# Six PSUM banks in the first round, and expert weights asked for earlier, in a Mamba-style decoder layer

## The chip, the cores and the metric

One core of a Trainium2 chip. The metric is the time of one execution on the device in microseconds (us). The core has five engines that run side by side and meet only at semaphores: TensorE (PE, matrix products, with PEld for its weight loads), VectorE (DVE), ScalarE (ACT), GpSimd (POOL) and SyncE (SP), which issues most of the DMAs. GpSimd issues the gathers, whose rows are chosen by numbers computed on the chip.

## The reference, cut to what matters

The input is x, 4 sequences of 256 tokens with 256 features, 1024 tokens in all. Three blocks follow one another, each with a residual sum and a layer norm:

```python
x = layernorm(x + mixer(x))        # 32 heads of 64, state 128; causal convolution of 4 taps
x = layernorm(x + context_ffn(x))  # 4 experts, chosen by token id
x = layernorm(x + routed_ffn(x))   # 16 experts of width 176, top 2 by router, and 1 shared

def mixer(x):
    x_ssm, z, B, C, dt_raw = split(x @ Win.T)
    dt = softplus(dt_raw + dt_bias)
    xc, Bc, Cc = silu(causal_conv(x_ssm)), silu(causal_conv(B)), silu(causal_conv(C))
    h_t = exp(-dt * exp(A_log)) * h_(t-1) + (dt * xc)_t B_t ;  y_t = h_t C_t
    y = y * rsqrt(mean(y * y) + 1e-6) * silu(z)
    return y @ Wout.T
```

## The kernel before, in words

**The mixer** runs in rounds, one for each pair of heads, 16 pairs. The recurrence is computed as masked attention over blocks of 128 tokens, with decays exp(cum_t - cum_s), where cum is the running sum of dt times the head's rate. A round n has a front and, one and two rounds later, a middle and a tail, so that `step(n, par, front, mid, tail)` of each engine works on three pairs at a time; `steps` calls it for round 0, round 1, a loop over rounds 2 to 15, and two closing rounds.

- Front, TensorE: `project(j)`, j = 0 to 11, is half j % 2 (512 tokens) of tile j // 2. Tiles 0 to 4 are x, B, C, B, C of the pair, tile 5 is the gate z. Each half is six matmuls (L793) into PSUM bank j % 4: the operands are split in a high and a low part. There are eight banks of 512; banks 4 and 5 take turned x and the scores, banks 6 and 7 the mixed output. Before it writes a bank again, TensorE waits in `half_read` until the half four before it has been read: by VectorE's taps, or for z by ScalarE.
- Front, ScalarE: `copy(j)` (L1251) takes a half out of PSUM times the last tap. VectorE: `tap(m, i)` (L1572) adds the three other taps of tile m; tile 0 in six instructions, tiles 1 to 4 in four each. Then ScalarE applies SiLU (L1236): tiles 0 to 3 at the end of its round, tile 4 in the next round, between copy(0) and copy(1), and z (L1242) there too.
- Middle: TensorE turns x to tokens (`x_to_tokens`, L776), scores (L807, L808) and `mix` (L821); GpSimd makes the arguments of the decays (`log_decay`, L477 and L483), ScalarE their exponentials (L1257), VectorE multiplies scores and decays (`weigh`, L1556).
- dt is made once, in round 0: TensorE projects it, ScalarE applies softplus, VectorE takes the running sum (`sum_dt`, L1510, ahead of tile 3's taps), SyncE stores it and loads it back broadcast (L339), TensorE turns dt and cum to tokens (`turn_dt`, L712), and VectorE copies both out (`take_dt`, L1516, L1517). In the kernel before, turning and taking stand between the steps of rounds 0 and 1, and TensorE waits for the copies (semaphore d_dtT) before round 1.

**The output projection** follows, with x1 stored in DRAM.

**The context experts** work on 11 blocks of up to 128 tokens (TBS = 11), sorted by expert. GpSimd gathers the rows of block j (L595); from the fourth on (AHEAD = 3) it waits until TensorE has turned block j - 3. For each block TensorE turns it (L946), multiplies with the chosen context (L955), turns the gate and multiplies again (L977); VectorE adds and takes the statistics. Blocks 0 to 7 (EARLY = 8) are normed by GpSimd (L617), blocks 8 to 10 by VectorE (L1777).

**SyncE's queue** in this stretch is an order written by hand: half of the experts' down weights (`load_down(0)`, L366, 88 partitions of 16 KB), the gate and up weights in four parts (L395, 128 partitions of 11 KB), then the 11 stores of the normed blocks x2 (L399), then the 11 stores of the residual (L403). Ahead of `load_down(0)` it waits for the gathers of all 11 blocks (`ld_row[j]`, L391).

**The shared expert** runs over the same 11 blocks while the router sorts the tokens: TensorE gate and up (L1061), ScalarE SiLU and a copy (L1407, L1412), GpSimd the product (`gate_shared`, L623), TensorE turns it (L1092) and multiplies down (L1111), and GpSimd adds the result to the residual (`add_residual`, L648). The first addition waits until all stores of x2 have landed, because it writes over their source. In the same queue of GpSimd stands the product that prepares the slot table (L655), which waits for VectorE's comparison (L1827). `slot_table` (L1031) on TensorE then gives each slot its token, VectorE writes the list (L1842, semaphore v_tab), and the routed gathers can start.

**The routed experts** work on 24 blocks. GpSimd gathers block j of x2 (`gather_block`, L630), from the fourth on after TensorE has turned block j - 3 (semaphore tx_done). ScalarE's first routed output waits for all 11 residual additions.

## Time and profile before

| | us |
|---|---|
| median of 3 runs | 696.69 (695.76 to 696.72) |
| the profiled execution, its own time | 696.84 |
| its span on the core | 695.1 |
| TensorE busy | 641.2, 92% |
| VectorE busy | 532.2, 77% |
| POOL, ScalarE busy | 475.6, 449.1 |
| mean granted TensorE clock | 0.965 of full |

The profile is of one execution. Times in it count from the start of the span; the 1.7 us between the span and the execution's own time lie around it. A row of a timeline gives start, duration, engine, line, operation, what is written and read, how often, and in brackets how long the engine had been idle and what ended it. The mixer takes the time up to about 500 us, the context experts 519 to 550, the shared expert and the router 550 to 591, the routed experts to 665, and the rest is the combination, the last norm and the stores.

### The profile page before, as it was taken

The page shows a single profiled execution, that of the slowest core. Times are in us where ns is not written, and L with a number is a line of the kernel's source. Part 1 is how long each engine was busy: PE and PEld are TensorE (multiplying, and loading weights), DVE is VectorE, ACT ScalarE, POOL GpSimd, SP SyncE. Part 2 cuts the span into 40 slices and gives each one's busy share as a digit, 9 for nine tenths or more (in the row PEclk, how much of TensorE's full clock was granted, in tenths as well). Part 3 has the DMA queues.
Part 4 walks back from the last instruction along what each step waited for, and adds up shares of the span by engine and source line. Part 5 has one row for each costly group of instructions (what it writes and reads, how often), then busy time and mean ns, then how long its engine had stood idle before and what let it go on. Part 6 is the DMA issues. An engine that isn't in the chain of part 4 may idle for free.

```text
span 695.1 us, 11898 instructions
## 1 busy us (share of the span) xinstructions
PE 641.2 (92%) x3514; PEld 492.9 (71%) x3514; DVE 532.2 (77%) x843; ACT 449.1 (65%) x722; POOL 475.6 (68%) x452
## 2 busy tenths in 40 slices
PE   7699999999999999999999999999998989899920
PEld 5477878878878888788788788788877766455510
DVE  5979999999999999999999999859644566122236
ACT  4657787887887887878878878874224544233321
POOL 4276779888898798798888987586515828444244
PEclk9989999999999999999999999999999999899965
DMA  4222112121131131111211211132252860587334
GB/s 154 90 93 98 62 49 64 42 106 60 46 106 60 46 105 60 47 65 49 99 60 46 106 60 45 56 96 83 69 128 73 233 273 14 143 250 205 90 83 129
DMA packets 25576, 65.07 MB, mean 94 GB/s; under 512 B 4148, under 2 KB 16948, under 8 KB 22812
## 3 DMA queue, kind: packets, MB, share of 16 engines
q1 hardware_dynamic: 22715, 56.96, 24.8%
q0 software_dynamic: 2832, 7.75, 4.3%
q8 instruction: 15, 0.25, 0.2%
q14 instruction: 14, 0.11, 0.1%
HBM read 56.42 MB, written 8.28 MB: 93 GB/s over the span
## 4 chain that ended last, share of the span: by engine, by line
PE 67%; DVE 12%; issue 6%; ACT 5%; DMA 4%; POOL 3%; SPq 2%; POOLq 0%; DVEq 0%; ACTq 0%
PE ps L793 27%; DVE conv L1572 8%; PE ps L821 7%; PE ps L807 5%; PE ps L1071 5%; PE ps L736 3%; PE ps L754 3%; ACT decay L1257 3%; PE ps L1115 3%; DVE decay L1556 3%; PE ps L808 2%; PE ps L776 2%; POOL conv L676 1%; SPq L399 1%; PE ps L955 1%
## 5 line engine op out<-in xcount | busy, mean ns | idle before, releaser
L1572 DVE SCALAR_TENSOR_TENSOR conv<-ps,w_raw,conv 128x506 f32<-128x506 f32 (+3 forms) x352 | 320.3, 933 | 16.9 <-ACT conv L1251 12.2
L793 PE MATMUL ps<-x_hi,w_hi 128*128 128x512 f32 x384 | 159.4, 415 | 6.7 <-DVE conv L1572 5.9
L793 PE MATMUL ps<-x_hi,w_lo 128*128 128x512 f32 x384 | 152.4, 397 | 1.0 <-DVE w_lo L1503 1.0
L1251 ACT ACTIVATE conv<-ps,w_raw 128x512 f32<-128x512 f32 x160 | 108.3, 686 | 69.4 <-PE ps L793 69.2
L793 PE MATMUL ps<-x_lo,w_hi 128*128 128x512 f32 x384 | 151.5, 394 | 0.0
L477 POOL TENSOR_TENSOR decay<-cum_b,cum_tok 128x512 f32<-128x512 f32 (+1 forms) x128 | 103.4, 830 | 15.1 <-DVE cum_tok L1517 15.1
L793 PEld LDWEIGHTS ps<-x_hi,w_hi 128*128 128x128 f32 x384 | 73.1, 190 | 25.5 <-DVE conv L1572 7.9
L483 POOL TENSOR_TENSOR decay<-decay,mask 128x512 f32<-128x512 f32 x64 | 82.5, 1289 | 5.0
L793 PEld LDWEIGHTS ps<-x_hi,w_lo 128*128 128x128 f32 x384 | 72.8, 189 | 18.1 <-DVE w_lo L1503 1.4
L793 PEld LDWEIGHTS ps<-x_lo,w_hi 128*128 128x128 f32 x384 | 73.1, 190 | 13.0
L807 PE MATMUL ps<-conv 128*128 128x256 f32 x256 | 79.5, 392 | 1.7 <-DVE decay L1556 0.3
L1236 ACT ACTIVATE conv<-conv 128x1024 f32<-128x1024 f32 x80 | 79.3, 1057 | 0.0
L1556 DVE TENSOR_TENSOR decay<-ps,decay 128x384 f32<-128x384 f32 x128 | 67.5, 547 | 7.8 <-PE ps L808 7.7
L492 POOL TENSOR_TENSOR y_all<-z_gate,y_all 128x512 f32 (+1 forms) x32 | 41.7, 1303 | 39.3 <-ACT y_all L1270 39.3
L497 POOL TENSOR_TENSOR y_lo<-y_sq,y_hi 128x512 fp32r<-128x512 f32 x32 | 41.5, 1297 | 36.9 <-ACT y_sq L1263 36.9
L1257 ACT ACTIVATE decay<-decay 128x768 f32<-128x768 f32 x64 | 52.0, 837 | 3.9 <-POOL decay L483 3.9
L808 PEld LDWEIGHTS ps<-conv 128*128 128x128 f32 x256 | 48.6, 190 | 6.6
L467 POOL TENSOR_TENSOR w_lo<-w_raw,w_hi 128x1536 fp32r<-128x1536 f32 x15 | 52.5, 3500 | 1.2
L807 PEld LDWEIGHTS ps<-conv 128*128 128x128 f32 x256 | 43.3, 189 | 12.6 <-DVE decay L1556 4.0
L808 PE MATMUL ps<-conv 128*128 128x128 f32 x256 | 49.2, 274 | 0.0
L821 PE MATMUL ps<-decay,xs 128*64 128x256 f32 (+1 forms) x512 | 48.9, 332 | 0.0
L465 POOL TENSOR_TENSOR w_hi<-w_raw,zero 128x1536 fp32r<-128x1536 f32 x15 | 41.2, 2749 | 7.8 <-DVE w_lo L1503 7.8
(259 smaller groups left out, 1095.0 us busy)
## 6 DMA issues: line engine op xcount, KB each, us to landing
cum_b<-cum_scratch SPq DMA_DIRECT2D x16, 1024.0 KB, 4.7
w_raw<-in_winT SPq DMA_DIRECT2D x16, 778.0 KB, 4.4
y_all<-in_wgu SPq DMA_DIRECT2D x4, 1408.0 KB, 19.2
ys_scratch<-y_blk SPq DMA_DIRECT2D x48, 64.0 KB
late<-in_wdn SPq DMA_DIRECT2D x2, 1408.0 KB
x_scratch<-conv SPq DMA_DIRECT2D x19, 128.0 KB, 7.4
late<-in_woutT SPq DMA_DIRECT2D x1, 2048.0 KB, 9.7
res_scratch<-conv SPq DMA_DIRECT2D x11, 130.0 KB
```

The costliest lines, as they stand in the source:

```text
L467: pool.tensor_tensor(w_lo[:, par, :], raw, w_hi[:, par, :].bitcast(F32), ALU.subtract).then_inc(S["w_split"], 1)
L477: pool.tensor_tensor(decay[:, 2 * b:2 * b + 2, c:t], cum_b[:, qp, :, b * T + j * P:(b + 1) * T], cum_tok[:, 2 * b + j, bass.ds(q * 2, 2)]. ...
L483: pool.tensor_tensor(diag, diag, mask[:, :].unsqueeze(1).unsqueeze(1).broadcast_to([P, 2, 2, P]), ALU.add).then_inc(S["p_arg"], 1)
L793: mm = pe.matmul(ps[:, j % 4, :], wp[:, par, w], xp[:, kk, t], start=(i == 0), stop=(i == 5))
L807: pe.matmul(ps[:, 4 + k % 2, 0:T], Bm[:, c0:c0 + P], Cm[:, c0:c0 + T], start=True, stop=True)
L808: pe.matmul(ps[:, 4 + k % 2, T:SC], Bm[:, c1:c1 + P], Cm[:, c1:c1 + P], start=True, stop=True).then_inc(S["s_done"], 1)
L821: mm = pe.matmul(ps[ch, 6 + g, (b % 2) * T + j * P:(b % 2) * T + T], xs[:, 2 * b + j, ch], decay[:, 2 * b + h, c:t], start=(j == 0), stop= ...
L1236: act.activation(conv[:, pp, tile, :], conv[:, pp, tile, :], ACT.Silu).then_inc(S["a_silu"], 1)
L1251: act.activation(conv[:, par, tile, hf * 512:(hf + 1) * 512], ps[:, j % 4, :], ACT.Copy, scale=w_raw[:, par, tap:tap + 1]).then_inc(S["a_c ...
L1257: act.activation(d, d, ACT.Exp).then_inc(S["a_decay"], 1)
L1556: dve.tensor_tensor(decay[:, k, :], ps[:, 4 + k % 2, 0:SC], decay[:, k, :], ALU.mult).then_inc(S["v_m"], 1)
L1572: dve.scalar_tensor_tensor(out=o[:, :, s:], in0=u[:, :, 0:T - s], scalar=w_raw[:, par, c:c + 1], in1=o[:, :, s:], op0=ALU.mult, op1=ALU.ad ...
```

## The change

Round 0 uses six PSUM banks for its tiles, and the turning of dt no longer stops TensorE between rounds 0 and 1; SyncE waits for four gathers where it waited for eleven; and GpSimd's residual additions 8 to 10 move behind the fourth routed gather. The core of the diff:

```diff
+        def tile_bank(n, tile):
+
+            return (0, 2, 6)[tile % 3] if isinstance(n, int) and n == 0 else 2 * tile % 4
...
-            for j in range(TBS):
+            for j in range(AHEAD + 1):
                 sp.wait_ge(ld_row[j], 16)
             load_down(0)
...
-            for j in range(AHEAD):
+            for j in range(NBLK):
                 gather_block(j)
                 if j == 0:
                     gate_shared(TBS - 1)
-                else:
-                    add_residual(TBS - 5 + j)
-            add_residual(TBS - 2)
-            add_residual(TBS - 1)
-            for j in range(AHEAD, NBLK):
-                gather_block(j)
+                elif j == 1:
+                    add_residual(TBS - 4)
+                elif j == 3:
+                    add_residual(TBS - 3)
+                elif j == 4:
+                    add_residual(TBS - 2)
+                    add_residual(TBS - 1)
                 if j >= 9 and j % 2 == 1 and j < 9 + 2 * TB:
                     gather_res((j - 9) // 2)
...
                 mm.then_inc(S["s_dtT"], 1)
-                pe.wait_ge(S["d_dtT"], 1)
...
                 def x_to_tokens(c):
                     ge(pe, S["a_silu"], q * NCONV + 1)
+                    if isinstance(q, int) and q == 0:
+                        pe.wait_ge(S["d_dtT"], 1)
...
                 def project(j):
-                    if j >= 4:
+                    if isinstance(n, int) and n == 0:
+                        if j >= 6:
+                            ge(pe, *half_read(n, j - 6))
+                    elif j >= 4:
                         ge(pe, *half_read(n, j - 4))
-                    elif not (isinstance(n, int) and n == 0):
+                    elif isinstance(n, int) and n == 1:
+                        ge(pe, *half_read(n - 1, j + 6))
+                    else:
                         ge(pe, *half_read(n - 1, j + 8))
...
-                            mm = pe.matmul(ps[:, j % 4, :], wp[:, par, w], xp[:, kk, t],
+                            mm = pe.matmul(ps[:, tile_bank(n, tile) + hf, :], wp[:, par, w], xp[:, kk, t],
...
                 def mix(p, b):
 
                     g = b // 2
+                    if isinstance(p, int) and p == 0:
+                        pe.wait_ge(S["a_z"], g + 1)
...
                 if isinstance(n, int) and n == 0:
                     between[3, 0] = [sum_dt]
+                    between[4, 0] = [take_dt]
...
-            steps(dve, step, take_dt)
+            steps(dve, step)
```

The readers of PSUM (ScalarE's `copy` and `z`, VectorE's `tap`) take `tile_bank` in the same way. In the changed kernel the line numbers are 4 to 13 higher.

VectorE at the end of round 0. Each L1572 or L1585 row is a tap of a tile; a row of 128x4x255 begins a tile, and 128x2x255 begins tile 0 of round 1. Before:

```order
21 L1572 SCALAR_TENSOR_TENSOR conv<-ps,w_raw,conv 128x4x255 [waits a_copy]
22 L1572 SCALAR_TENSOR_TENSOR conv<-ps,w_raw,conv 128x4x254 [waits v_tap]
23 L1572 SCALAR_TENSOR_TENSOR conv<-ps,w_raw,conv 128x2x253 [waits v_tap] x2
24 L1516 COPY dt_tok<-ps 128x256 [waits s_dtT]
25 L1517 COPY cum_tok<-ps 128x256
26 L1572 SCALAR_TENSOR_TENSOR conv<-ps,w_raw,conv 128x2x255 [waits a_copy,d_dtT]
```

Changed:

```order
21 L1529 COPY dt_tok<-ps 128x256 [waits s_dtT]
22 L1530 COPY cum_tok<-ps 128x256
23 L1585 SCALAR_TENSOR_TENSOR conv<-ps,w_raw,conv 128x4x255 [waits a_copy,d_dtT]
24 L1585 SCALAR_TENSOR_TENSOR conv<-ps,w_raw,conv 128x4x254 [waits v_tap]
25 L1585 SCALAR_TENSOR_TENSOR conv<-ps,w_raw,conv 128x2x253 [waits v_tap] x2
26 L1585 SCALAR_TENSOR_TENSOR conv<-ps,w_raw,conv 128x2x255 [waits a_copy]
```

The two copies have moved ahead of tile 4's four taps.

GpSimd where the routed gathers begin (L630 or L634 is a gather, L648 or L652 a residual addition, L623 or L627 the last shared product). Before:

```order
245 L630 DMA xb<-x_scratch,y_all 128x256 [waits v_tab]
246 L623 TENSOR_TENSOR h_tok<-h_tok,u_tok 128x176 [waits a_u]
247 L630 DMA xb<-x_scratch,y_all 128x256
248 L648 TENSOR_TENSOR conv<-conv,y_blk 128x256 [waits a_y]
249 L630 DMA xb<-x_scratch,y_all 128x256
250 L648 TENSOR_TENSOR conv<-conv,y_blk 128x256 [waits a_y] x3
251 L630 DMA xb<-x_scratch,y_all 128x256 [waits tx_done] x7
```

Changed:

```order
247 L634 DMA xb<-x_scratch,y_all 128x256
248 L652 TENSOR_TENSOR conv<-conv,y_blk 128x256 [waits a_y]
249 L634 DMA xb<-x_scratch,y_all 128x256
250 L634 DMA xb<-x_scratch,y_all 128x256 [waits tx_done]
251 L652 TENSOR_TENSOR conv<-conv,y_blk 128x256 [waits a_y]
252 L634 DMA xb<-x_scratch,y_all 128x256 [waits tx_done]
253 L652 TENSOR_TENSOR conv<-conv,y_blk 128x256 [waits a_y] x2
254 L634 DMA xb<-x_scratch,y_all 128x256 [waits tx_done] x5
```

Of the three additions that stood ahead of the fourth gather, one now follows it and two follow the fifth.

## Rows read from the trace of the kernel before

**Rows 1.** The page: busy time, share and instructions of each engine.

```profile
PE 641.2 (92%) x3514; PEld 492.9 (71%) x3514; DVE 532.2 (77%) x843; ACT 449.1 (65%) x722; POOL 475.6 (68%) x452
```

**Rows 2.** Timeline of VectorE, 26 to 75 us: end of round 0, starts of rounds 1, 2.

```profile
28.48 7.95 DVE L1572 SCALAR_TENSOR_TENSOR conv<-ps,w_raw,conv 128x1020 f32<-128x1020 f32 x8
37.66 0.42 DVE L1516 COPY dt_tok<-ps 128x256 f32<-128x256 f32 x1 [1.23 <-PE ps L712]
...
41.79 3.75 DVE L1572 SCALAR_TENSOR_TENSOR conv<-ps,w_raw,conv 128x510 f32<-128x510 f32 x5 [3.38 <-ACT conv L1251]
...
67.64 3.75 DVE L1572 SCALAR_TENSOR_TENSOR conv<-ps,w_raw,conv 128x510 f32<-128x510 f32 x5 [0.51 <-ACT conv L1251]
```

**Rows 3.** Timeline of TensorE, 28 to 75 us: the eleventh half of round 0.

```profile
31.90 0.60 PE L793 MATMUL ps<-x_hi,w_hi 128*128 128x512 f32 x1 [3.36 <-DVE conv L1572]
```

**Rows 4.** Timeline of SyncE's queue, 470 to 600 us: weights and stores of x2.

```profile
540.37 0.32 SPq L366 DMA_DIRECT2D late<-in_wdn  x1
...
543.63 23.07 SPq L399 DMA_DIRECT2D x_scratch<-conv  x11
```

**Rows 5.** Line 399, the stores of x2: time of issue in ns, then the landing.

```profile
L399 SPq DMA_DIRECT2D x_scratch<-conv x11: 320/432/6506, 543.6 to 566.3; - x11
...
DMA to landing us min/median/max: 4.6/14.2/20.3
```

**Rows 6.** Timeline of GpSimd, 505 to 605 us: gathers (L595, L630), addition (L648), product (L655).

```profile
523.14 0.95 POOL L595 DMA_INDIRECT conv<-x_scratch,cum_b  x1 [0.61 <-PE ps L946]
...
526.96 0.95 POOL L595 DMA_INDIRECT conv<-x_scratch,cum_b  x1 [1.19 <-PE ps L946]
...
532.64 0.95 POOL L595 DMA_INDIRECT conv<-x_scratch,cum_b  x1 [1.22 <-PE ps L946]
...
571.30 0.72 POOL L648 TENSOR_TENSOR conv<-conv,y_blk 128x256 f32<-128x256 f32 x1 [5.91 <-DMA x_scratch<-conv]
...
575.95 2.60 POOL L655 TENSOR_TENSOR y_all<-y_all,cum_b 128x1056 bf16<-128x1056 f32 x1
...
586.34 1.06 POOL L630 DMA_INDIRECT xb<-x_scratch,y_all  x1 [0.55 <-DVE y_all L1842]
...
593.66 0.96 POOL L630 DMA_INDIRECT xb<-x_scratch,y_all  x1 [0.16 <-issue]
```

**Rows 7.** Timeline of TensorE, 549 to 606 us: shared expert, slot table, third routed block.

```profile
573.61 0.42 PE L1092 MATMUL ps<-ident,h_tok 128*88 128x128 f32 x2 [3.26 <-POOL h_tok L623]
...
584.72 0.88 PE L1031 MATMUL ps<-y_all,conv 128*64 128x48 bf16 x44
...
595.83 0.69 PE L1045 MATMUL ps<-ident,xb 128*128 128x128 f32 x2 [1.72 <-DMA xb<-x_scratch,y_all]
```

**Rows 8.** Timelines of GpSimd and ScalarE, 26 to 75 us: decay arguments and exponentials.

```profile
38.55 1.61 POOL L477 TENSOR_TENSOR decay<-cum_b,cum_tok 128x512 f32<-128x512 f32 x2 [15.09 <-DVE cum_tok L1517]
...
48.70 1.57 ACT L1257 ACTIVATE decay<-decay 128x768 f32<-128x768 f32 x2
```

**Rows 9.** Timeline, 0 to 45 us: SyncE asks for the running sums.

```profile
30.45 0.81 SPq L339 DMA_DIRECT2D cum_b<-cum_scratch  x2
```

**Rows 10.** The page, DMA issues: count, size, median us from issue to landing.

```profile
cum_b<-cum_scratch SPq DMA_DIRECT2D x16, 1024.0 KB, 4.7
```

**Rows 11.** DMA queues, 518 to 540 us: packets, MB, share; then landing.

```profile
q0 software_dynamic: 528, 1.44, 23.8%
...
conv<-x_scratch,cum_b POOLq DMA_INDIRECT x11, 3.3
```

**Rows 12.** Timeline of VectorE, 564 to 700 us: the comparison that the product at 575.95 needs.

```profile
571.32 1.83 DVE L1827 TENSOR_TENSOR y_all<-y_all,cum_b 128x1056 f32<-128x1056 int32 x1
```

**Rows 13.** DMA queues, 540 to 570 us, weights and stores: packets, MB, share.

```profile
q1 hardware_dynamic: 2237, 8.63, 87.6%
```

**Rows 14.** Busy time by stretch: PE, PEld, DVE, ACT, POOL; then clock, DMA share, GB/s.

```profile
546.00:552.00 6.00, 6.00 (x40) 5.27 (x39) 3.32 (x11) 2.19 (x5) 4.79 (x15) 1.00 1.01 223
552.00:558.00 6.00, 5.30 (x33) 3.86 (x31) 2.37 (x6) 5.57 (x11) 4.80 (x6) 1.00 0.99 410
```

More of the change, by code:

```diff
@@ L1241, in z @@
                         ge(act, S["v_y"], q * 2 - 2)
-                    act.activation(z_gate[:, qp, hf * 512:(hf + 1) * 512], ps[:, (2 * NCONV + hf) % 4, :], ACT.Silu
+                    act.activation(z_gate[:, qp, hf * 512:(hf + 1) * 512], ps[:, tile_bank(q, NCONV) + hf, :], ACT.Silu
                                    ).then_inc(S["a_z"], 1)
@@ L1250, in copy @@
                     tap = KD * PW + tile * TAPS + TAPS - 1
-                    act.activation(conv[:, par, tile, hf * 512:(hf + 1) * 512], ps[:, j % 4, :], ACT.Copy,
+                    act.activation(conv[:, par, tile, hf * 512:(hf + 1) * 512], ps[:, tile_bank(n, tile) + hf, :], ACT.Copy,
                                    scale=w_raw[:, par, tap:tap + 1]).then_inc(S["a_copy"], 1)
@@ L1568, in tap @@
                     o = conv[:, par, m, :].rearrange("p (b t) -> p b t", b=NB)[:, 2 * halves.start:2 * halves.stop, :]
-                    u = ps[:, (2 * m) % 4:(2 * m) % 4 + 2, :].rearrange("p a (b t) -> p (a b) t", b=2)
+                    u = ps[:, tile_bank(n, m):tile_bank(n, m) + 2, :].rearrange("p a (b t) -> p (a b) t", b=2)
                     u = u[:, 2 * halves.start:2 * halves.stop, :]
```

## The prediction

> **What bounds the kernel now.** I read the page first: TensorE is busy for 641.2 of 695.1 us, VectorE for 532.2 [rows 1]. A share near full says little about an edit, so I went to the two places the diff touches and asked there which wait ends last.
>
> The first is the hand-over from round 0 of the mixer (the first pair of heads) to round 1. VectorE runs round 0's last eight taps from 28.48 to 36.43, copies the turned step sizes out of PSUM (37.66 to 38.41, two copies of 0.42 us that overlap a little), and then stands still: its first tap of round 1 is at 41.79 [rows 2]. In between TensorE turns dt and waits for those copies before it projects anything of round 1. TensorE, for its part, stood idle for 3.36 us before 31.90, waiting for taps to free a PSUM bank, and came back at a matmul of 0.60 us [rows 3]. From 41.79 on VectorE has no gap until 67.64, where it waits 0.51 us for ScalarE [rows 2]: a start of round 1 that is earlier on VectorE is earlier for everything behind it, round by round.
>
> The second is the stretch from the context experts to the routed ones. SyncE holds the 7 MB of expert weights (one of 1408 KB, then four) until all eleven context gathers have landed, at 540.37, and puts the eleven stores of x2 behind them in the same queue, from 543.63 to 566.7 [rows 4]. A store takes up to 20.3 us to land, and one took 6.51 us to issue, since the queue was full [rows 5]. The chain that ended last runs straight through this issue. GpSimd's first residual addition waits for it, 5.91 us, until 571.30 [rows 6]; the shared expert's products queue behind it, and TensorE idles 3.26 us before 573.61 [rows 7].
>
> **The change, part by part.**
>
> *Six banks in round 0, dt turned without a stop.* No matmul, copy or tap is added or removed. With six banks TensorE's seventh to twelfth half of round 0 wait for taps two halves older; VectorE was never the one that waited there, so its taps still end when they did: 36.43, plus the two copies, now between tile 3 and tile 4 (37.66 to 38.41, 0.75 us). That is 37.2. Round 1's first two halves need only tile 3's taps (about 32) and run while VectorE does tile 4. Even at the slow clock's 0.43 us per matmul the first is done by 34.5, so ScalarE's copy is there before 37.2. The second copy stands behind a SiLU that needs tile 4's last tap: 37.2 + 1.06 + 0.69 = 39.0, and VectorE wants it after three taps of 0.75 us, at 39.5. So VectorE's first tap moves from 41.79 to 37.2: **-4.6 us**. Who could be late next? GpSimd's decay arguments of round 0 started at 38.55, on VectorE's copy [rows 8]; now they can start when the cumulative sums are back, which SyncE asks for at 30.45 and has 4.7 us later [rows 9, 10], at 35.2, 3.3 us earlier. That is less than 4.6, but ScalarE takes the first pair, ready 2.9 us after GpSimd's start, only at 48.70 [rows 8]: cover enough. The z wait that the change puts ahead of the first mix is met about 20 us before it. Bounds: -3.5 (if a slow clock holds round 1's third and fourth half, which VectorE meets by 42.2) to -5.0.
>
> *Weights behind four gathers: what it frees.* The fourth gather is issued at 523.14 [rows 6] and lands 3.3 us later [rows 11], so the weights start at 526.5 instead of 540.4, 13.9 us earlier. The first store stood behind all of them and landed at 543.6 + 20.3 = 563.9, so they are in by about 550 now, and the last x2 store goes out as soon as its block is normed. GpSimd's first addition no longer waits; but not all of the 5.91 us comes back. The product at 575.95 (2.60 us) waits for VectorE's comparison that ends at 573.15 [rows 12], whatever the stores do; it then starts 2.8 us earlier, the shared expert's loop of 2.27 us per block follows it, and the slot table, at 584.72 and long waited for [rows 7], comes at about 581.6. So the first routed gather, 586.34 [rows 6], moves by **-3.1 us**. Bounds: -1.5 to -5.9.
>
> *What it costs.* Six gathers, of blocks 5 to 10, now fly among 7 MB of weights. No row of before shows a gather beside a backlog like that. What the rows do show: eleven gathers made 528 packets [rows 11], 48 each, three on each of the 16 DMA engines; the weights and stores made 2237, one for each row [rows 13]. While the down weights move, in rows of 16 KB, the queues carry 223 GB/s, and later, with gate and up in rows of 11 KB, 410 [rows 14]: 1.2 and 0.44 us for a row on one engine. If each packet of a gather waits for one row of weights, a gather costs 3 x 1.2 = 3.6 us more in the first stretch (some 10 us, 528 to 540 with the gathers' own time) and 1.3 in the second. Gather 5 is issued at 526.96 and lands at 530.3; block 5 has been turned when gather 8 goes out, at 532.64 [rows 6], so its slack is 1.9 us, and 2.7 for the later ones. Gather 5 comes at 533.9, 1.7 late. Gather 6 follows 3.6 + 0.5 us behind, at 538.0, where 534.3 was needed: 3.7. Gather 7 is at 541.0 for 536.5: 4.5. After that a gather takes 1.8 us in a cadence of 2.17 (1.22 idle and 0.95 of issue [rows 6]) and no more is lost. Everything behind is **+4.5 us** later. The lower end is 0: later, among copies of expert weights, 18 gathers never made TensorE wait. The upper end is every gather held until the weights are in: 550 against 534.3, +16. I take the middle reading, since it rests on counted packets.
>
> At this place a rule of the Trainium skill speaks against the change. The Trainium skill, page "DMA: Bandwidth & Descriptors", section "Queues, rings and completion order", has an engine drain a packet of typically 9 to 17 descriptors from one ring before it turns to another. By that rule the wait at each turn would be a whole load's share, and the sum would end above the time before; the packet counts of this trace, one per row, speak for the shorter turn, and no row here shows the two queues both backed up.
>
> *Fourth routed gather ahead of three additions.* It was issued at 593.66 [rows 6], behind three additions of 0.7 us each; it will go out about 1.8 us earlier. TensorE waits there for the third gather alone, 1.72 us before 595.83 [rows 7]; the fourth lands at 597.0 as it is, while TensorE is still at the third's work. The delayed additions have room too, as ScalarE's first routed output, which waits for them, comes some 7 us later. I cost it at **0**, bounds -0.3 and +0.3; if the third gather came earlier, the fourth would be next.
>
> Sum: -4.6 - 3.1 + 4.5 + 0 = **-3.2 us**. Against the profiled execution's own 696.84 (span 695.1, 1.7 around it) that is 693.6; the median of the runs is 0.15 lower, so 693.5.
>
> **The rivals.**
> 1. *Gathers are not held up* (below 1.5 us): -7.7, 689.0. For it: the later gathers among weight copies. Against: those copies are 528 KB at a time, with pauses, not 7 MB in a row.
> 2. *Whole loads go first*, the slower side. Place: blocks 5 and 6 of the context experts. If each of gather 5's three packets waits for a load's share (1408 KB at 223 GB/s is 6.3 us, at 410 it is 3.4), it lands at 530.3 + 13.1 = 543.4; gather 6 waits for the other two and lands near 550.3, where 534.3 was needed: +16, so 696.7 - 7.7 + 16 = 705.0. It decides once the loss passes 9.1 us. The rule of the Trainium skill above would do this.
> 3. *In between* (6.3 to 9.1 us lost): within 0.2% of before.
> 4. *The bank edit does not pay*, because some wait keeps VectorE's second round at 41.79: 693.5 + 4.6 = 698.1. I see no such wait.
>
> **How the numbers follow.** Forecast (loss of 1.5 to 6.3 us) 0.50; rival 1 0.20; rival 2 0.17; rival 3 0.10; rival 4 0.03. A measurement of this kernel can tell about 0.2%, 1.4 us, from no change. Faster: 0.50 + 0.20 = 0.70. Same: 0.10 + 0.03 = 0.13. Slower: 0.17. The range goes from 688.8 (all gain, nothing lost) to 699.5, which takes in rivals 3 and 4 and the mild end of rival 2; most of rival 2 and bank gains beyond the sum are left out. The forecast's own range is 690.5 to 695.3.
>
> **What would show it.** VectorE's first tap of round 1 near 37.2, and the context stage starting 4.6 us earlier. The weights' issue some 14 us earlier still, right behind the fourth gather. Gather landings of 5 to 8 us in place of 3.3, with TensorE waiting for them between blocks 5 and 8; 3.3 would be rival 1, over 12 rival 2. No wait of GpSimd for an x2 store, and TensorE's 3.26 us gone. It is wrong if round 2 does not start 4.6 us earlier, or if the product at 575.95 moves by less than the stores do.

## The result and the profile after

The changed kernel is slower. Its median is 699.15 us (19 runs, 696.15 to 704.69) against 695.25 us (19 runs, 691.61 to 698.18) of the kernel before on the same chips; the ratio is 1.0066, 95% interval 1.0048 to 1.0084. Of 695.25 us that is 4.6 us more (the two medians differ by 3.9). The forecast was 3.2 us less. Put on the 696.69 us that it started from, the measured ratio gives 701.3, where it had 693.5 and a range up to 699.5. The profiled execution of the changed kernel happens to be one of its quick ones: 697.0 us, span 695.1, the same span as in the profile of before. So the trace shows a draw, in which a gain and a loss cancel, and the loss of the median has to be found with the experiments.

The page's busy times answer to [rows 1]:

```profile
PE 638.4 (92%) x3514; PEld 490.8 (71%) x3514; DVE 531.6 (76%) x843; ACT 449.7 (65%) x722; POOL 475.1 (68%) x452
```

**The start of round 1.** VectorE's timeline of the changed kernel (start, duration, engine, line, operation, count, idle before). Tap code is at L1585 now, the copies at L1529 and L1530:

```profile
33.13 0.42 DVE L1529 COPY dt_tok<-ps 128x256 f32<-128x256 f32 x1
33.46 0.42 DVE L1530 COPY cum_tok<-ps 128x256 f32<-128x256 f32 x1
33.91 7.68 DVE L1585 SCALAR_TENSOR_TENSOR conv<-ps,w_raw,conv 128x1020 f32<-128x1020 f32 x9
41.51 0.68 DVE L1560 TENSOR_TENSOR xs<-ps,dt_tok 128x512 f32<-128x512 f32 x1
...
63.65 3.75 DVE L1585 SCALAR_TENSOR_TENSOR conv<-ps,w_raw,conv 128x510 f32<-128x510 f32 x5 [0.51 <-ACT conv L1264]
```

The nine taps at 33.91 are the last four of round 0 and the first five of round 1, without a gap between them; the first one of round 1 begins at 37.85, where the forecast had 37.2. The standstill of 3.38 us before 41.79 [rows 2] is gone. The wait for ScalarE that stood at 67.64 is at 63.65.

**The context stage.** GpSimd's context gathers (L599) of the changed kernel. The first is at 515.04, where it was at 518.87 before; the sixth, of block 5, is the one at 522.34:

```profile
515.04 1.18 POOL L599 DMA_INDIRECT conv<-x_scratch,cum_b  x1 [21.86 <-DMA x_scratch<-conv]
...
522.34 0.95 POOL L599 DMA_INDIRECT conv<-x_scratch,cum_b  x1 [0.67 <-PE ps L959]
...
526.99 0.95 POOL L599 DMA_INDIRECT conv<-x_scratch,cum_b  x1 [1.22 <-PE ps L959]
535.70 0.95 POOL L599 DMA_INDIRECT conv<-x_scratch,cum_b  x1 [7.76 <-PE ps L959]
539.40 0.95 POOL L599 DMA_INDIRECT conv<-x_scratch,cum_b  x1 [2.75 <-PE ps L959]
541.56 0.95 POOL L599 DMA_INDIRECT conv<-x_scratch,cum_b  x1 [1.22 <-PE ps L959]
```

SyncE and TensorE beside them:

```profile
522.38 0.32 SPq L370 DMA_DIRECT2D late<-in_wdn  x1
522.74 2.83 SPq L399 DMA_DIRECT2D y_all<-in_wgu  x4
```

```profile
534.74 0.69 PE L959 MATMUL ps<-ident,conv 128*128 128x128 f32 x2 [6.08 <-DMA conv<-x_scratch,cum_b]
```

The weights are queued 0.04 us after gather 5 was begun. TensorE then stands for 6.08 us, and GpSimd, which waits for TensorE before it can issue gather 8, for 7.76. The chain of work that ended last has the gather's own time (start, duration, what), and the answer for line L599 the landings of all eleven:

```profile
522.34 12.36 DMA conv<-x_scratch,cum_b
534.70 0.04 issue
534.74 0.69 PE ps L959 x2
```

```profile
DMA to landing us min/median/max: 2.7/6.3/12.4
```

Before, all eleven took 3.3 us. The wait has a second price: TensorE's clock fell to half during it (532 to 538, rows at the end of this document), so block 5 took 4.0 us from its turn at 534.74 to the next one, where a block takes 2.2. From the first context gather to the last it was 536.97 - 518.87 = 18.1 us; it is 541.56 - 515.04 = 26.5 now, so 8.4 us were lost where the forecast had 4.5.

How the two queues shared the DMA engines can be read from the single packets. A gather is 48 of them: 32 rows of 4 KB and 16 closing packets of 4 bytes, so two rows and a closing packet on each of 16 engines. Gather 4, issued at 520.73, has its packets from 522.43 to 523.12. Gather 5, issued at 522.34, begins its first row only at 529.07. The queues (kind: packets, MB, share of 16 engines) from 523.2 to 529, and then from 529 to 532.6; q1 carries the weights and q0 the gathers:

```profile
q1 hardware_dynamic: 83, 1.22, 94.0%
```

```profile
q1 hardware_dynamic: 54, 0.72, 87.4%
q0 software_dynamic: 52, 0.15, 19.6%
```

First weights alone moved, then about one packet of weights for each packet of a gather. The records do not name the engine of a packet, but each begins where another one ends. Joined that way, most engines that carry w_dn read: five rows of w_dn, a row of the gather, a row of w_dn, a row of the gather, a row of w_dn, the gather's closing packet, a row of w_dn. Gather 5 lost 5.0 us before its first row (it began 6.7 us after the issue, gather 4's 1.7 us), 2.8 in the turns from first to last packet (3.5 against 0.7), and 1.8 until the last of its sixteen landing signals, one from each engine. Fifteen of them had come by 533.58; the one at 534.70 is from an engine where a packet of 16 KB of instructions (queue q8) had come in between.

**From there to the routed experts.** GpSimd's first residual addition, the shared expert's product and the first routed gather, to be laid beside [rows 6]:

```profile
571.12 0.73 POOL L652 TENSOR_TENSOR conv<-conv,y_blk 128x256 f32<-128x256 f32 x1
...
579.44 2.53 POOL L659 TENSOR_TENSOR y_all<-y_all,cum_b 128x1056 bf16<-128x1056 f32 x1 [1.93 <-DVE y_all L1841]
...
589.24 1.06 POOL L634 DMA_INDIRECT xb<-x_scratch,y_all  x1 [0.55 <-DVE y_all L1856]
```

The addition has no wait for a store any more (5.91 us before). But the product that follows now waits for VectorE. From the last context gather to the first routed one it is 47.7 us, after 49.4, so 1.7 us less. Most of that is the clock: before, TensorE was at half its clock for 3.4 us of this stretch (from 574.9), and in the changed kernel never. The kernel with the order alone (below), which has no relief of the stores and no such fall, needs 48.0, and the one with early weights alone, with relief and a fall of 3.4 us, needs 49.3. At like clock, as far as single traces can tell, 0.1 to 0.3 of the 5.91 us are left. VectorE's comparison, which the product waits for, starts 36.5 us behind the last context gather (578.10), where it was 34.4 (571.32).

**The routed stage** is 2.9 us shorter than before (695.1 - 589.24 = 105.9 against 108.8). The granted clock goes with it. TensorE's stretches (busy time and count of each engine, then PEclk, DMA share, GB/s), of before and then of the changed kernel:

```profile
596.00:598.00 2.00, 1.60 (x6) 0.66 (x8) 0.00 (x0) 0.38 (x1) 0.95 (x1) 0.50 1.00 270
598.00:600.00 2.00, 2.00 (x9) 0.76 (x6) 0.07 (x1) 0.32 (x1) 0.00 (x0) 0.50 0.51 162
600.00:602.00 2.00, 2.00 (x9) 0.92 (x9) 0.69 (x2) 0.38 (x1) 0.94 (x1) 0.50 0.00 0
```

```profile
596.00:598.00 2.00, 1.57 (x10) 0.50 (x6) 0.34 (x1) 0.52 (x2) 1.83 (x3) 1.00 0.93 264
598.00:600.00 2.00, 1.09 (x8) 0.50 (x8) 0.00 (x0) 0.19 (x1) 1.84 (x3) 1.00 0.82 241
600.00:602.00 2.00, 1.41 (x10) 0.56 (x8) 0.56 (x2) 0.70 (x2) 1.04 (x2) 1.00 0.73 209
```

Before, TensorE had stood for 1.72 us at 595.83 [rows 7] and then ran 6 us at 1.2 GHz, with matmuls of 0.79 us in place of 0.46. The changed kernel stood twice for 0.2 to 0.3 us there and kept 2.4 GHz. The other traces bear this out: the nine of the experiments below without such a fall near its start have 104.6 to 105.7 us for it, whatever the order of the gathers, and those with a fall of 3.4 us 105.7 to 107.8.

### The profile page after: what moved, and what is told of

Same layout as the page of the kernel before. It is cut to its first block, busy times and chain, and to the rows that moved or that the text cites. A ratio compares the mean times of both kernels' runs of the same rounds, so it can differ in the third digit from the quotient of the medians.

```text
span 695.1 us, 11898 instructions
## 1 busy us (share of the span) xinstructions
PE 638.4 (92%) x3514; PEld 490.8 (71%) x3514; DVE 531.6 (76%) x843; ACT 449.7 (65%) x722; POOL 475.1 (68%) x452
## 4 chain that ended last, share of the span: by engine, by line
PE 66%; DVE 13%; issue 6%; DMA 6%; ACT 5%; POOL 3%; SPq 0%; POOLq 0%; DVEq 0%; ACTq 0%
PE ps L804 26%; DVE conv L1585 8%; PE ps L834 7%; PE ps L818 5%; PE ps L1084 4%; PE ps L740 3%; PE ps L758 3%; ACT decay L1270 3%; DMA conv<-x_scratch,cum_b 3%; PE ps L1128 3%; DVE decay L1569 3%; PE ps L819 2%; PE ps L782 2%; POOL conv L681 2%; PE ps L1058 1%
## 5 line engine op out<-in xcount | busy, mean ns | idle before, releaser
L1585 DVE SCALAR_TENSOR_TENSOR conv<-ps,w_raw,conv 128x506 f32<-128x506 f32 (+3 forms) x352 | 320.7, 935 | 13.7 <-ACT conv L1264 9.0
L481 POOL TENSOR_TENSOR decay<-cum_b,cum_tok 128x512 f32<-128x512 f32 (+1 forms) x128 | 103.4, 830 | 11.7 <-DMA cum_b<-cum_scratch 11.7
L818 PEld LDWEIGHTS ps<-conv 128*128 128x128 f32 x256 | 43.2, 189 | 13.6 <-issue 4.3
```

Of the source, the lines that this page charges most:

```text
L481: pool.tensor_tensor(decay[:, 2 * b:2 * b + 2, c:t], cum_b[:, qp, :, b * T + j * P:(b + 1) * T], cum_tok[:, 2 * b + j, bass.ds(q * 2, 2)]. ...
L818: pe.matmul(ps[:, 4 + k % 2, 0:T], Bm[:, c0:c0 + P], Cm[:, c0:c0 + T], start=True, stop=True)
L1585: dve.scalar_tensor_tensor(out=o[:, :, s:], in0=u[:, :, 0:T - s], scalar=w_raw[:, par, c:c + 1], in1=o[:, :, s:], op0=ALU.mult, op1=ALU.ad ...
```

## The experiments

Each was timed in five rounds beside the kernel before; "ratio" is to that kernel, with its 95% interval. The parts of the change are taken first one at a time.

**The bank and dt edit alone.**

```diff
 # the change's diff without these two places:
-            for j in range(AHEAD + 1):
+            for j in range(TBS):
                 sp.wait_ge(ld_row[j], 16)
 # and with the gathers and residual additions in their old order
```

> The kernel before with the bank and dt edit alone; loads and order as before. Theory A (the forecast's terms for banks and stores are right, and the early weights cost more than all of them): 4.0 to 4.6 us faster than before, ratio 0.993 to 0.994. Theory B (the early start of round 1 is given back further on, for instance at the context gathers, and the weights are innocent): ratio 0.999 to 1.001.

688.71 us, ratio 0.9952 (0.9937 to 0.9968), so -3.3 us, between -4.4 and -2.2. In its trace VectorE's wait for ScalarE is at 63.45, after 67.64 in [rows 2], and the first context gather at 514.72, 4.15 us earlier:

```profile
63.45 3.75 DVE L1584 SCALAR_TENSOR_TENSOR conv<-ps,w_raw,conv 128x510 f32<-128x510 f32 x5 [0.51 <-ACT conv L1263]
```

```profile
514.72 1.17 POOL L599 DMA_INDIRECT conv<-x_scratch,cum_b  x1 [21.91 <-DMA x_scratch<-conv]
```

Of the 4.15 us, 3.2 are left at the first routed gather (583.18, after 586.34). The gain of the first part is there and most of it stays, about 1 us less than theory A had. Theory B falls.

**Early weights alone.**

```diff
 # before.py
-            for j in range(TBS):
+            for j in range(AHEAD + 1):
                 sp.wait_ge(ld_row[j], 16)
             load_down(0)
```

> The kernel before with SyncE's wait cut to four context gathers, nothing else. Theory A: the sixth context gather lands 12 to 13 us after its issue and the context stage ends 8 to 9 us later; x2's stores give 3 back; 6 to 11 us slower than before, ratio 1.008 to 1.016. Theory B: ratio 0.998 to 1.002. By the forecast's own terms (+4.5 and -3.1) it would be 1.002.

703.32 us, ratio 1.0138 (1.0086 to 1.0190): +9.6 us, between 6.0 and 13.1, with the relief of the stores already in it. Its trace repeats that of the changed kernel: the longest landing is 12.9 us, TensorE stands 7.46 us before block 5.

```profile
526.66 0.95 POOL L595 DMA_INDIRECT conv<-x_scratch,cum_b  x1 [0.30 <-PE ps L946]
```

```profile
526.87 0.32 SPq L366 DMA_DIRECT2D late<-in_wdn  x1
```

```profile
539.62 0.69 PE L946 MATMUL ps<-ident,conv 128*128 128x128 f32 x2 [7.46 <-DMA conv<-x_scratch,cum_b]
```

**The order of gathers and additions alone.**

```diff
 # before.py
-            for j in range(AHEAD):
+            for j in range(NBLK):
                 gather_block(j)
                 if j == 0:
                     gate_shared(TBS - 1)
-                else:
-                    add_residual(TBS - 5 + j)
-            add_residual(TBS - 2)
-            add_residual(TBS - 1)
-            for j in range(AHEAD, NBLK):
-                gather_block(j)
+                elif j == 1:
+                    add_residual(TBS - 4)
+                elif j == 3:
+                    add_residual(TBS - 3)
+                elif j == 4:
+                    add_residual(TBS - 2)
+                    add_residual(TBS - 1)
```

> The kernel before with the order of routed gathers and residual additions alone. The forecast's term: 0, within 0.3 us, ratio 0.9995 to 1.0005. Rival, since the routed stage of the changed kernel ran 2.9 us shorter from the first routed gather to the end (105.9 against 108.8 us): the order is worth up to 2.9 us, ratio 0.996. If it is 1.000, those 2.9 us are from the transfers' and the clock's state there, not from the order.

693.13 us, ratio 1.0020 (0.9993 to 1.0047). No gain; between -0.5 and +3.3 us. Its one profiled execution has a span of 692.2 us, 2.9 less than before, yet its median is not below; a single span is no measure of an edit of this size. In this trace the wait of GpSimd at the first residual addition (5.40 us, at 571.07) ends with ScalarE's copy and not with a store.

**The changed kernel with all loads late.**

```diff
 # after.py
-            for j in range(AHEAD + 1):
+            for j in range(TBS):
                 sp.wait_ge(ld_row[j], 16)
```

> The changed kernel with SyncE's wait put back to all eleven context gathers: banks and order alone. Theory A: 4 to 5 us faster than before, ratio 0.993 to 0.994, and so 8 to 9 us faster than the changed kernel; POOL waits 5 to 6 us for a store of x2 again. Theory B: ratio 1.000 to 1.005 against before.

687.49 us, ratio 0.9927 (0.9897 to 0.9958), -5.1 us. Against the changed kernel's 1.0066 this one line is worth 1.4%, 9.6 us, the same as when it was added alone. From either side the early weights cost some 9.6 us net (the intervals leave 6 to 13), and with them late the change would have been a gain. GpSimd's wait for a store, expected at 5 to 6 us, was 1.04 us in the profiled execution of this run.

Next: what in those 7 MB holds the gather up?

**The loads turned round.**

```diff
 # after.py
-            load_down(0)
             n_gu = NE * KD * GW // 4
             for c in range(4):
                 sp.dma_start(w_gu[:, c * n_gu:(c + 1) * n_gu], wgu[:, c * n_gu:(c + 1) * n_gu]
                              ).then_inc(S["ld_gu"], 16)
+            load_down(0)
```

> The changed kernel with its five loads turned round: four of w_gu (128 rows of 11 KB each) first, then the one of w_dn (88 rows of 16 KB). Theory L (the load that is in the queue ahead of gather 5 goes whole before the gather's first packet; that is 6.3 us for 1408 KB at the 223 GB/s of w_dn, 3.4 us at the 410 GB/s of w_gu): the longest gather landing falls from 12.4 to 9 or 10 us, TensorE's wait from 6.1 to about 3, ratio against before 1.001 to 1.003. Theory S (it is the sum of what is queued, 7 MB in either order, that counts): landing 12 us and ratio 1.006 as the changed kernel.

702.01 us, ratio 1.0110 (1.0069 to 1.0150). Both theories missed the time, and the profiled execution (706.05) is the slowest of the six. The wait at block 5 is as theory L said, but a second stands at block 10, where w_dn now goes by, and the longest landing is 11.3 us:

```profile
532.66 0.69 PE L959 MATMUL ps<-ident,conv 128*128 128x128 f32 x2 [2.91 <-DMA conv<-x_scratch,cum_b]
549.24 0.69 PE L959 MATMUL ps<-ident,conv 128*128 128x128 f32 x2 [4.50 <-DMA conv<-x_scratch,cum_b]
```

What decides is which load is in front of which gather, more than the first load alone.

**Only w_dn early.**

```diff
 # after.py
             load_down(0)
             n_gu = NE * KD * GW // 4
+            for j in range(AHEAD + 1, TBS):
+                sp.wait_ge(ld_row[j], 16)
```

> The changed kernel with only the load of w_dn behind the fourth gather; the four of w_gu wait for the eleventh again, x2's stores behind them. Theory L: gather 5 lands about 9 to 10 us after its issue, since its first packet waits for the whole of w_dn as before and the other two for nothing; TensorE waits about 3 to 4 us; ratio against before 0.997 to 1.001. Theory S (the backlog of 7 MB counts): landing 4 to 5 us, no TensorE wait over 1 us, ratio 0.993 as with all loads late.

696.84 us, ratio 1.0049 (1.0021 to 1.0077). Both theories missed it. That is 8.5 us over the kernel with all loads late: a fifth of the bytes makes nearly all of the loss. TensorE stands as long as with all five:

```profile
533.69 0.69 PE L961 MATMUL ps<-ident,conv 128*128 128x128 f32 x2 [6.62 <-DMA conv<-x_scratch,cum_b]
```

The queues tell why. In the stretches 522 to 534 and 534 to 544 (queue, kind: packets, MB, share of 16 engines) q1 carries the load and q0 the gathers:

```profile
q1 hardware_dynamic: 99, 1.44, 52.3%
q0 software_dynamic: 184, 0.50, 16.2%
```

```profile
q0 software_dynamic: 136, 0.38, 13.6%
```

The load, with no other weights about, is in flight until 533 or 534, some 12 us, and not the 6.3 that 1408 KB at 223 GB/s came to. The 223 GB/s of [rows 14] were not the rate of w_dn alone. Gather 5 landed 12.1 us after its issue. Five of its sixteen landing signals came by 525.75, the other eleven between 531.83 and 533.65. That fits a load whose 88 rows lie on eleven engines, eight on each: on the five others the gather's rows went at once (from 524.35), on the eleven they stood behind w_dn's first rows and then took turns with the rest.

**Only the first load of w_gu early.**

```diff
 # after.py
             for j in range(AHEAD + 1):
                 sp.wait_ge(ld_row[j], 16)
+            load_gu(0)              # the first of the four, as its own call
+            for j in range(AHEAD + 1, TBS):
+                sp.wait_ge(ld_row[j], 16)
             load_down(0)
-            # four loads of w_gu
+            # the other three
```

> The changed kernel with only the first load of w_gu behind the fourth gather, all others behind the eleventh. Theory L: gather 5 lands 6.5 us after its issue (3.3 and half the 3.4 us to 3.4 us of the load ahead), which the three gathers of lead mostly cover: TensorE waits under 1 us and the ratio is 0.993 to 0.996. A ratio over 0.998 would say that one load of this size holds a gather up for longer than it takes itself.

689.62 us, ratio 0.9955 (0.9921 to 0.9988), within theory L's bounds. The longest landing is 6.3 us and TensorE stands 1.01 us, at 531.30. The stretch 525 to 528.3 of its queues:

```profile
q1 hardware_dynamic: 97, 1.09, 92.6%
q0 software_dynamic: 9, 0.00, 0.4%
```

Gather 5 was issued at 524.91. Landing in 3.3 us it would have been complete at 528.2, yet up to 528.3 q0 moved only nine small packets, the end of the gather before, while q1 moved 97. Its first row began at 528.94. In the changed kernel it is the same picture in 523 to 528, behind w_dn, where a gather of 3.3 us would have been complete at 525.6:

```profile
q1 hardware_dynamic: 66, 0.97, 88.2%
q0 software_dynamic: 7, 0.00, 0.1%
```

So the gather's first row does not share with the load ahead, it stands behind a run of its rows.

**w_dn by partitions, 80 and 8.**

```diff
 # after.py, load_down(0)
-                sp.dma_start(w_dn[:, 0:n], wdn[:, 0:n])
+                for a, z in ((0, 80), (80, 88)):
+                    sp.dma_start(w_dn[a:z, 0:n], wdn[a:z, 0:n])
 # TensorE waits for the counts of three loads, not two
```

> The changed kernel with the early load of w_dn cut by partitions into rows 0 to 79 and rows 80 to 87. Reading of the earlier runs (theory E): the 88 rows of 16 KB go to 11 of the 16 DMA engines, 8 rows each at 1.2 us, so one load keeps those engines for 9.6 us, while 80 rows would go to 16 engines, 5 each, 6 us. Then the longest gather landing falls from 12.4 to 9 or 10 us and TensorE's wait at block 5 from 6.1 to 3 to 4: ratio 1.001 to 1.004, and the rate behind the issue rises above 223 GB/s. Rival: the rate of w_dn is a property of its rows however they are spread: landing 12 us, ratio 1.006.

697.94 us, ratio 1.0054 (1.0025 to 1.0083); TensorE stands 5.97 us at block 5. Theory E expected half of that, and a landing of 9 or 10 us where the longest was 11.5. Spreading the same rows differently does not help, as the rival said. The single packets show why: an engine now has five rows of the first load, and again five rows go ahead of the gather's first one, which begins at 527.04, 6.3 us after its issue.

**w_dn by columns, four loads with rows of 4 KB.**

```diff
 # after.py, load_down(0)
-                sp.dma_start(w_dn[:, 0:n], wdn[:, 0:n])
+                for c in range(4):
+                    at = slice(c * n // 4, (c + 1) * n // 4)
+                    sp.dma_start(w_dn[:, at], wdn[:, at])
 # TensorE waits for the counts of five loads, not two
```

> The changed kernel with the early load of w_dn cut by columns into four loads of 88 rows of 4 KB. Theory N (the queue gives way to a gather after a number of rows, eight of one load, whatever their size): the first packet of gather 5 waits 8 x 0.3 = 2.4 us in place of about 6, landing 7 to 8 us, TensorE waits under 2, ratio 0.998 to 1.001. Theory B (it is the bytes ahead that count): landing 12 us, ratio 1.006.

696.07 us, ratio 1.0027 (0.9995 to 1.0060). TensorE stands much less before block 5, and once more before block 7:

```profile
529.31 0.44 PE L964 MATMUL ps<-ident,conv 128*128 128x128 f32 x2 [1.57 <-DMA conv<-x_scratch,cum_b]
...
533.17 0.44 PE L964 MATMUL ps<-ident,conv 128*128 128x128 f32 x2 [0.80 <-DMA conv<-x_scratch,cum_b]
```

Gather 5, issued at 522.20, was used 7.1 us later, as theory N said, and first to last context gather is 536.73 - 514.99 = 21.7 us in place of 26.5. The same bytes in shorter rows hold the gather up for less: its first row began 3.0 us after the issue, where it was 6.7 in the changed kernel. Gather 6 still took 9.2 us. The median came down by 0.4% from the changed kernel, less than that suggests; its interval takes in the upper end of theory N. Where the rest is lost is open.

**Stores among the loads.**

```diff
 # after.py: all loads wait for range(TBS); then w_dn, two loads of w_gu, and
             for j in range(TBS):
                 sp.wait_ge(*normed(j))
                 sp.dma_start(x2_dram[j * P:(j + 1) * P, :], xg[:, j, :]).then_inc(S["st_x2"], 16)
+                if j in (2, 5):
+                    load_gu(2 + j // 5)
```

> The changed kernel with all loads behind the eleventh gather and x2's stores taken out from behind them: w_dn and two loads of w_gu, three stores, the third load, three stores, the fourth, five stores. If the stores' place behind the loads costs what the forecast said (3.1 us), it is 2 to 4 us faster than the kernel with all loads late: ratio against before 0.988 to 0.991, and GpSimd's first residual addition has no wait for a store. Rival: ScalarE's and VectorE's part of the shared expert decides there anyway, ratio 0.992 to 0.994.

686.93 us, ratio 0.9912 (0.9881 to 0.9944). The time lies between the forecast (0.988 to 0.991) and the rival (0.992 to 0.994), and its interval overlaps that of the kernel with all loads late (0.9927). A gain from the stores is not shown here, and the expected sign did not come: GpSimd still waits for a store, behind the last load.

```profile
565.56 0.72 POOL L657 TENSOR_TENSOR conv<-conv,y_blk 128x256 f32<-128x256 f32 x1 [5.78 <-DMA x_scratch<-conv]
```

**The stores alone.**

```diff
 # before.py: w_dn and two loads of w_gu, the eleven stores of x2, then
+            for c in range(2, 4):
+                load_gu(c)
```

> The kernel before with x2's eleven stores put ahead of the last two loads of w_gu and nothing else: the forecast's term of -3.1 us by itself. Forecast: GpSimd's 5.9 us at the first residual addition goes, ratio 0.9945 to 0.997. Rival: ScalarE's copies for the same addition, which end the wait in the trace of another kernel with the late stores, arrive as late, ratio 0.999 to 1.001.

691.03 us, ratio 0.9969 (0.9941 to 0.9998), -2.2 us, between -4.1 and -0.1. GpSimd's first addition has no wait for a store:

```profile
571.14 0.72 POOL L653 TENSOR_TENSOR conv<-conv,y_blk 128x256 f32<-128x256 f32 x1
```

But it is hardly earlier than the 571.30 of before, and the first routed gather is later, at 590.95. This execution (698.36) is the slowest of the twelve, with 13.6 us at half clock between the last context gather and the first routed one, so it cannot show where the median's 2.2 us come from. The rival, ScalarE's copies, is not excluded by it.

**Banks and stores.**

```diff
 # the bank and dt edit alone, and with it
+            for c in range(2, 4):
+                load_gu(c)
 # behind the eleven stores, the first two loads ahead of them
```

> The kernel before with the bank and dt edit and with x2's stores ahead of the last two loads of w_gu; loads behind the eleventh gather, routed gathers in their old order. If both terms add (3.3 measured for the banks, 1 to 3 for the stores): ratio 0.990 to 0.993, as good as or better than the kernel with stores among the loads (0.991). If the stores give nothing: 0.995 as with the banks alone.

688.15 us, ratio 0.9919 (0.9881 to 0.9957), as expected if both terms add; the interval just reaches the 0.995 of the banks alone. Four kernels with all loads late, this one, the one with stores among the loads (0.9912), the changed kernel with SyncE's old wait (0.9927) and the bank edit alone (0.9952), beat both the kernel before and the changed one. Their intervals overlap, and none is shown to be better than the others.

## Why the prediction was wrong

**Six banks, forecast -4.6.** Right in its mechanism. The first context gather is 3.8 us earlier in the changed kernel and 4.15 with the edit alone; over all traces it lies at 513.9 to 517.0 with the edit (ten) and at 518.9 to 519.7 without (four), 4.7 between the middle values. In the medians of the edit alone it is -3.3 (-4.4 to -2.2). Part of what misses in its trace is at the very start: ScalarE could read its first w_raw at 8.93 there and at 8.44 before. No cover that the text named gave way: ScalarE's first decay pair moved from 48.70 [rows 8] to 42.93.

**Weights earlier, forecast -3.1 for the stores.** The wait of 5.91 us went, as said, and the stores taken alone measured -2.2 (-4.1 to -0.1). In the traces nearly nothing comes through: at like clock 0.1 to 0.3 us with early weights. With early weights alone the first addition is 29.5 us behind the last context gather, where it was 34.3, and the first routed gather is 49.3 behind, where it was 49.4. The forecast let VectorE's comparison stay where it was and end at 573.15; it came 2.1 to 2.2 us later, counted from the last context gather, and took the gain. The forecast's own sign of being wrong, a product that moves by less than the stores, came. The median of the stores alone and the traces do not agree on the size of this term, and that stays open.

**The context gathers, forecast +4.5.** This is the step that failed: "if each packet of a gather waits for one row of weights, a gather costs 3 x 1.2 = 3.6 us more". The price of a row held (the median of w_dn's was 1.13 to 1.25 us, by the trace), and so did the turns of one row, once the gather's first row had gone. What the sum put at nothing is the run in front of that first row: five rows of w_dn, so that the gather's closing packet stood behind seven rows of an engine's eight, where the rule had three. Gather 5 took 12.4 us where the rule gave 6.9; 5.0 of the 9.7 us that it took longer than gather 4 are that run. Why five rows went first is open. A second term put at nothing is the clock: TensorE's fell during the wait, and block 5 at half speed cost another 1.8 us (4.0 against 2.2). The gathers behind came better than forecast: 6 and 7 landed 1.6 us apart from the one before, where the sum had 4.1 and 3.0.

The load's whole time is not the rule either, though 12.1 and 12.4 us look like it: seven of eight rows is nearly all of a load. With 80 and 8 rows the five rows of the first load were through before the gather's first one, and it still took 11.5 us. Only the price that rival 2 and theory L set on a load was wrong in itself: 6.3 us for w_dn came from a stretch, 546 to 552 [rows 14], in which w_gu moved too. Its rows took 10.2 us from first to last there (541.29 to 551.49), and 11.1 to 11.7 with gathers between them. (1408 KB are 1.44 MB in these views, so that the two rates give 6.5 and 3.5 us, not 6.3 and 3.4.) From first to last context gather 8.4 us went in the changed kernel and 9.0 with early weights alone (546.79 - 519.72 = 27.1), and net of what the stores give back the line costs 9.6 us in the medians, where the forecast had 1.4.

**The rivals.** The slower side was rival 2, whole loads go first. Its sign, a landing over 12 us, came; its place is right for block 5, though TensorE had no wait at block 6; and so is its side of the deciding point: with the forecast's gains of 7.7 us a result of +4.6 is a loss of 12.3, over 9.1, and under its 16. With the gains as measured (3.3 and 2.2) the loss is some 10. Its mechanism is only half right: a long run goes first, but the turns behind it are single rows, so its price was too high, 705.0 against 699.15. The forecast's short turns and rival 2's long ones each describe one part of the same gather. The packet counts were read as evidence for short turns. They only say how many rows there are, not in which order an engine takes them. The Trainium skill, page "DMA: Bandwidth & Descriptors", section "Queues, rings and completion order", has an engine drain 9 to 17 descriptors typically before it changes rings. The run ahead of the gather's first row goes in that direction, five rows of w_dn, and seven or all eight of an engine's rows with one load of w_gu early. The turns behind it do not: there the trace of the changed kernel has single rows.

**The fourth routed gather, forecast 0.** Measured -0.5 to +3.3 alone, and -1.7 between the two kernels with banks, loads late, and either order (0.9927 and 0.9952, with intervals that overlap). It is not told apart from 0; the forecast's bounds of 0.3 were narrower than can be measured. The 2.9 us by which the routed stage shortened aren't the order's: with early weights alone, in the old order, that stage is as short (701.6 - 596.05 = 105.6).

## What to carry to other kernels

Before moving bulk loads ahead of small, latency-bound transfers, ask how many rows of the load an engine gets and how long one takes. Charge the small transfer's first packet a run of them (here five rows of 16 KB, or six to eight of 11 KB), and each further packet one row. With eight rows on an engine and three packets that comes to nearly the whole load. Compare it with the slack that the reader has, and add what the clock costs if the reader is TensorE and stands. Bulk can be started early with little harm only if that slack covers it: here one load of 3.4 us ahead cost some 2 us and one of 12 us cost 8.5, against all loads late. Otherwise let it wait. Whether stores that another engine waits for should come out from behind the bulk has to be tried: the wait goes, but here another operand came hardly earlier, and the gain (2.2 us, between 0.1 and 4.1) is barely told from none.

## What the runs showed of the hardware

- A load of 1408 KB in 88 rows of 16 KB took some 12 us from its issue with no other load beside it, 11.1 from first to last row; the loads of w_gu, as large but in 128 rows of 11 KB, moved 1.09 MB in 3.3 us. In the records of the kernel with only w_dn early up to eleven of its rows are in flight at a time, some 1.1 to 1.2 us each; with the rows cut into 80 and 8 it is some sixteen, each about as slow, and the wait behind them was hardly shorter. Why a row of 16 KB takes 1.2 us where one of 11 KB takes 0.43 was not tried. The two tensors differ in more than the row: in DRAM the rows lie 32 KB apart in one and 44 KB in the other.
- With two queues backed up, the indirect one moved no row on an engine until a run of the other's rows had gone (to 529.07 in the changed kernel, five rows of 16 KB; to 528.94 behind one load of w_gu, seven or eight rows of 11 KB). Then the engine took the two in turn, row by row. Smaller rows ahead made the first wait shorter.
- TensorE's granted clock makes single executions a poor measure here. Spans were 695.1 before and 692.2 with the order alone, where the medians are level; the kernel with w_gu first ran at a granted clock of 0.960 in its profile, the one with stores among the loads at 0.977. The fall to 1.2 GHz at 595.4 before came in the wait of 1.72 us that ended at 595.83. In the changed kernel it fell during the wait of 6.08 us at block 5 and stayed down behind it:

```profile
532.00:534.00 2.00, 0.00 (x0) 0.00 (x0) 0.00 (x0) 0.00 (x0) 0.00 (x0) 0.50 1.01 218
534.00:536.00 2.00, 1.09 (x4) 0.72 (x5) 0.00 (x0) 0.38 (x1) 0.30 (x1) 0.50 0.99 372
536.00:538.00 2.00, 2.00 (x7) 1.64 (x6) 0.00 (x0) 0.39 (x1) 0.65 (x1) 0.50 0.95 398
538.00:540.00 2.00, 2.00 (x12) 1.73 (x12) 1.41 (x4) 1.05 (x3) 0.60 (x1) 1.00 0.99 417
```

(stretches of the changed kernel, columns as above). The block after the wait was computed at half speed, four matmuls in 1.91 us in place of 1.03, which adds to the cost of the wait itself.
